# Contextual attention on one core: a third PSUM bank for the paste, other chunk widths, the shifted add on GpSimd, features ahead of masks

## The reference, cut to what matters

```python
raw_w = extract_patches(b, 4, 2)              # 1600 patches of 64 x 4 x 4
f = b[:, :, ::2, ::2]                         # 40 x 40
w = extract_patches(f, 3, 1)                  # 1600 patches of 64 x 3 x 3
mm = (mean of the mask patch == 0)
norm = sqrt(sum(w * w)); wn = w / maximum(norm, 1e-4)
yi = einsum('bpd,bld->blp', w, wn) * mm       # scores, l: patch, p: place
yi = softmax(yi * 10, axis=l) * mm
patches = einsum('blp,bld->bpd', yi, raw_w)
out = overlap-add of the patches with stride 2, cut by 1, / 4
```

## Time and profile before

| | us |
|---|---|
| runs, median (lowest, highest) | 1791.49 (1788.55, 1794.37) |
| profiled execution, its own time | 1782.45 |
| its span | 1780.6 |
| PE busy | 1591.8 |
| DVE busy | 1090.1 |
| ACT busy | 901.4 |
| POOL busy | 51.2 |
| mean granted TensorE clock | 0.952 |

### The profile page before, as it was taken

One profiled execution on the slowest core, in us unless ns is written; L12 is line 12 of the kernel. 1 busy time (PEld: TensorE's weight loads), 2 busy tenths in 40 slices (PEclk: granted clock), 3 DMA queues, 4 the chain that ended last, 5 costly groups with the idle time before them and its releaser, 6 DMA issues.

```text
span 1780.6 us, 27285 instructions
## 1 busy us (share of the span) xinstructions
PE 1591.8 (89%) x7260; PEld 1052.2 (59%) x7260; DVE 1090.1 (61%) x2526; ACT 901.4 (51%) x2265; POOL 51.2 (3%) x62
## 2 busy tenths in 40 slices
PE   3887899998999899998999989999899989999986
PEld 3756566665666566565665656666566656656543
DVE  5224555675566756576656755667556676667784
ACT  1446454574446744565535645457344573457431
POOL 1000100001000000000000010000100000000100
PEclk9987899999999999998999999999889999999998
DMA  3400624226422445225352262422633234522342
GB/s 61 62 1 12 143 61 89 72 70 139 84 63 72 104 111 106 55 69 124 86 96 61 66 145 66 92 72 73 137 71 77 72 94 109 106 64 66 112 122 78
DMA packets 181701, 149.64 MB, mean 84 GB/s; under 512 B 120016, under 2 KB 177424, under 8 KB 181520
## 3 DMA queue, kind: packets, MB, share of 16 engines
q1 hardware_dynamic: 181522, 147.62, 35.1%
HBM read 19.78 MB, written 13.11 MB: 18 GB/s over the span
## 4 chain that ended last, share of the span: by engine, by line
PE 71%; DVE 10%; ACT 8%; issue 7%; SPq 2%; DMA 1%; DVEq 0%; ACTq 0%; POOL 0%; POOLq 0%
PE psG L433 35%; PE psO L449 30%; DVE S L723 4%; ACT S L575 3%; PE psG L428 3%; DVE G L773 2%; PE psM L347 2%; ACT G L565 2%; ACT OSB L595 1%; ACT G L586 1%; PE psB L362 1%; SPq L251 1%; DVE Z L806 1%; DVE G L784 1%; ACT SQ L529 1%
## 5 line engine op out<-in xcount | busy, mean ns | idle before, releaser
L449 PE MATMUL psO<-Z,B 123*128 123x492 f32 (+2 forms) x1792 | 786.5, 569 | 66.7 <-ACT OSB L595 57.9
L723 DVE CUSTOM_DVE_ANT_0 S<-psG,RB 123x369 f32<-123x369 f32 (+1 forms) x448 | 267.4, 605 | 547.3 <-PE psG L433 471.0
L565 ACT ACTIVATE G<-psG 123x369 f32<-123x369 f32 (+1 forms) x448 | 236.6, 529 | 695.8 <-DVE mx L723 693.9
L449 PEld LDWEIGHTS psO<-Z,B 123*128 123x128 f32 x1792 | 335.9, 199 | 301.3 <-issue 202.3
L433 PE MATMUL psG<-LH,HL 128*123 128x369 f16 (+3 forms) x2592 | 474.8, 329 | 26.2 <-issue 13.8
L433 PEld LDWEIGHTS psG<-LH,HL 128*123 128x123 f16 x2592 | 338.0, 138 | 175.3 <-issue 94.9
L586 ACT ACTIVATE G<-G,nb 123x492 f32<-123x492 f32 (+1 forms) x448 | 268.2, 646 | 125.5 <-DVE G L773 125.1
L575 ACT ACTIVATE S<-S,nm 123x360 f32<-123x360 f32 (+3 forms) x560 | 306.3, 551 | 0.1
L773 DVE SCALAR_TENSOR_TENSOR G<-G,RA,psB 123x492 f32<-123x492 f32 (+1 forms) x448 | 275.4, 658 | 21.8 <-issue 18.2
L784 DVE TENSOR_TENSOR G<-G,SH 123x492 f32<-123x492 f32 (+1 forms) x448 | 251.2, 601 | 14.7 <-DMA SH<-G 14.5
L806 DVE TENSOR_TENSOR Z<-G 123x984 f32<-123x984 f32 (+2 forms) x192 | 209.8, 1093 | 30.4 <-PE psO L449 30.3
(11 more groups left out here) (74 smaller groups left out, 515.2 us busy)
## 6 DMA issues: line engine op xcount, KB each, us to landing
SH<-G SPq DMA_DIRECT2D x224, 214.8 KB
SH<-G SPq DMA_DIRECT2D x224, 161.0 KB
XP<-x SPq DMA_DIRECT2D x20, 280.0 KB, 5.5
XP<-mid SPq DMA_DIRECT2D x20, 280.0 KB, 5.4
SH<-G SPq DMA_DIRECT2D x224, 19.2 KB
HL<-SQ SPq DMA_DIRECT2D x16, 246.5 KB, 3.3
LH<-SQ SPq DMA_DIRECT2D x16, 246.5 KB, 4.5
SH<-G SPq DMA_DIRECT2D x224, 14.4 KB
```

The lines of the kernel that those rows point to most:

```text
L449: last = pe.matmul(psO[:, b, 0:n], B[:, o:o + 128], Z[:, 2 * (s % 2) + j, 0:n], start=t == 0, stop=t == TILES - 1)
L565: act.activation(G[:, t * GLEN + c0:t * GLEN + c0 + n], psG[0:TW, par, 0:n], ACT.Copy).then_inc(g_read, 1)
L723: dve.tensor_tensor_reduce(S[:, par, 0:n], psG[0:TW, par, 0:n], RB[:, s0 * TW:s0 * TW + n], 1.0, 0.0, ALU.mult, ALU.max, mx[:, par:par + 1 ...
```

## The change

Chunk widths become 3, 4, 4, 3 for the paste and 2, 4, 4, 4 for the scores. Scores start in slot 3 instead of 2; slots 17, 18 and 21 have two pairs, slots 2, 28 and 29 none. `psO` gets three banks and `psM` one. A chunk's two accumulations use the banks of `O_BANK`; from the second chunk on b = 0 has a bank that is free and b = 1 waits only for the first of the two reads of the chunk before. Between images (chunk 3 to chunk 0) the banks are the same two, and each b waits for its own. `read_out` moves ahead of `softmax_pair`. The patch copies of ACT come one slot later, and all users of `psM` follow one another in its one bank; `scale_rows` is spread over the end of the pass (g = 0) and slots 3, 4 and 5. `add_shifted` moves from DVE to POOL, with no slot of its own: POOL waits for each DMA in turn. On DVE `sum_pair` goes first in a slot. Four feature tensors become one tensor `PK`, and six DMAs lay it out instead of eight. `low_features(0)` goes ahead of the mask work.

```diff
-P_CHUNKS = [(0, 4), (4, 4), (8, 3), (11, 3)]
-S_CHUNKS = [(0, 3), (3, 4), (7, 3), (10, 4)]
+P_CHUNKS = [(0, 3), (3, 4), (7, 4), (11, 3)]
+S_CHUNKS = [(0, 2), (2, 4), (6, 4), (10, 4)]
-AHEAD = 2
 def score_list(s):
-    if s < 16:
-        return [s - FIRST]
-    if s < 21:
-        return [14, 15] if s == 16 else [s - 1]
-    if s < SLOTS:
-        return [20, 21] if s == 21 else [s]
-    return []
+    if s < 3 or s >= SLOTS:
+        return []
+    if s < 17:
+        return [s - 3]
+    if s < 22:
+        return [[14, 15], [16, 17], [18], [19], [20, 21]][s - 17]
+    return [s]
...
-        psO = ps("psO", [128, 2, 512])
+        psO = ps("psO", [128, 3, 512])
-        psM = ps("psM", [128, 2, 512])
+        psM = ps("psM", [128, 512])
+        O_BANK = [(2, 1), (0, 2), (1, 0), (2, 1)]
...
-                for dst, src in ((HL[0:64, :], HS), (HL[64:128, :], LS), (LH[0:64, :], LS), (LH[64:128, :], HS),
-                                 (H1[0:64, :], HS), (H1[64:128, 0:n - 1], HS[:, 1:n]),
-                                 (HV[0:64, :], HS), (HV[64:128, 0:n - TW], HS[:, TW:n])):
+                for dst, src in ((PK[0:64, 0:3, :], HS.unsqueeze(1).to_broadcast([64, 3, n])), (HL[64:128, :], LS),
+                                 (LH[0:64, :], LS), (LH[64:128, :], HS),
+                                 (H1[64:128, 0:n - 1], HS[:, 1:n]), (HV[64:128, 0:n - TW], HS[:, TW:n])):
...
         def scale_rows(u, v, g):
             pe.wait_ge(r_step, (v + 1) * R_STEPS)
-            if g == 0 and u is not None:
+            if g > 0:
                 pe.sem_inc(pe_gate, 1)
-                pe.wait_ge(b_made, u * PAIRS + 4)
-            if g == 2 and u is not None:
+                pe.wait_ge(r_rows, v * 4 + g)
+            elif u is not None:
                 pe.sem_inc(pe_gate, 1)
                 pe.wait_ge(b_made, (u + 1) * PAIRS)
-            if g in (1, 3):
-                pe.sem_inc(pe_gate, 1)
-                pe.wait_ge(r_rows, v * 4 + (1 if g == 1 else 2))
...
         def paste_tile(at, s, j):
-                    if i == 0:
-                        pe.wait_ge(o_read, (u * NK + k + 1) * 2)
...
                 for b in range(2):
+                    if t == 0:
+                        pe.sem_inc(pe_gate, 1)
+                        pe.wait_ge(o_read, (u * NK + k) * 2 + b + (2 if k == 0 else 1))
                     o = (2 * t + b) * 128
-                    last = pe.matmul(psO[:, b, 0:n], B[:, o:o + 128], Z[:, 2 * (s % 2) + j, 0:n],
+                    last = pe.matmul(psO[:, O_BANK[k][b], 0:n], B[:, o:o + 128], Z[:, 2 * (s % 2) + j, 0:n],
                                      start=t == 0, stop=t == TILES - 1)
...
         # ACT, body
-                    at = place(u, v, s + LEAD)
+                    if u is not None and s % PAIRS == 0 and s <= SLOTS:
+                        read_out(u, s // PAIRS - 1)
                     if s == 24 and v is not None:
                         lse_log(v, False)
-                    elif at:
+                    at = place(u, v, s + LEAD)
+                    if at and s != 24:
                         softmax_pair(at)
-                    if u is not None and s % PAIRS == 0 and s <= SLOTS:
-                        read_out(u, s // PAIRS - 1)
+                    if v is not None and (NK - 1) * PAIRS < s <= SLOTS:
+                        block_group(u, v, s - 1 - (NK - 1) * PAIRS)
...
         # DVE, body
+                    at = place(u, v, s + 1)
+                    if at:
+                        sum_pair(at, s + 1)
+                    at = place(u, v, s + LEAD)
+                    if at and s != 24:
                         argument_pair(at)
-                    at_y = place(u, v, s + AHEAD)
-                    if at_y:
-                        add_shifted(at_y)
-                    at_z = place(u, v, s + 1)
-                    if at_z:
-                        sum_pair(at_z, s + 1)
...
         # POOL
+                    pool.wait_ge(sh_in[o % SFREE], (u * (NB // SFREE) + o // SFREE + 1) * 16 * len(SHIFT_PARTS))
+                    g = G[:, t * GLEN + c0:t * GLEN + c0 + n]
+                    pool.tensor_tensor(g, g, SH[:, o % SFREE, 0:n], ALU.add).then_inc(y1_made, 1)
...
             def body(u, v):
                 for s in BODY:
+                    at = place(u, v, s + LEAD)
+                    if at:
+                        add_shifted(at)
```

More of the change, by code:

```diff
@@ L72, in contextual_attention @@
         G = sb("G", [TW, TILES * GLEN], F32)
[L73 to L76, removed]
+        PK = sb("PK", [128, 4, FLEN], F16)
+        HL, H1, HV, LH = (PK[:, i, :] for i in range(4))
         XP = sb("XP", [128, TILES * STRIPS, 2 * PITCH], F32)
@@ L343, in row_squares @@
                 if v is not None:
-                    pe.wait_ge(r_rows, v * 4 + 3)
+                    pe.wait_ge(r_rows, v * 4 + 4)
                 for r in range(FROWS):
-                    last = pe.matmul(psM[0:TW, Q_BANK, r:r + 1], SQ[0:64, r * TW:(r + 1) * TW], ones[:, :],
+                    last = pe.matmul(psM[0:TW, r:r + 1], SQ[0:64, r * TW:(r + 1) * TW], ones[:, :],
                                      start=True, stop=True)
@@ L395, in block_group @@
                     pe.sem_inc(pe_gate, 1)
[L397 to L402, removed]
+                if g > 0:
+                    pe.wait_ge(b_made, v * PAIRS + g)
+                elif w is not None:
+                    pe.wait_ge(r_step, w * R_STEPS + 4)
                 else:
-                    pe.wait_ge(b_made, v * PAIRS + g)
+                    pe.wait_ge(r_rows, v * 4 + 4)
                 for t in (2 * g, 2 * g + 1):
@@ L408, in block_group @@
                         o = (t % 2 * 2 + b) * 128
-                        last = pe.transpose(psM[0:TW, BLOCK_BANK[g], o:o + 128], xt, idn[:, :])
+                        last = pe.transpose(psM[0:TW, o:o + 128], xt, idn[:, :])
                 last.then_inc(blk_psum, 1)
@@ L457, in body @@
                     pairs = score_list(s) if v is not None else []
-                    if s == 4 and v is not None:
-                        scale_rows(u, v, 2)
-                        scale_rows(u, v, 3)
+                    if 3 <= s <= 5 and v is not None:
+                        scale_rows(u, v, s - 2)
                     if s == 5 and u is not None:
@@ L464, in body @@
                         lse_row(u, 3)
-                    if s == FIRST and v is not None:
+                    if pairs and pairs[0] == 0:
                         pe.wait_ge(f_in, (v + 1) * N_F * 16)
@@ L482, in body @@
                         block_group(v, w, s - 21)
-                    if w is not None and s in (25, 26):
-                        scale_rows(v, w, s - 25)
+                if w is not None:
+                    scale_rows(v, w, 0)
                 if v is not None:
@@ L489, in _ @@
             for t in range(TILES):
-                last = pe.matmul(psM[0:TW, 0, 2 * t:2 * t + 2], G[0:LAYERS, MASK_AT + t * TW:MASK_AT + (t + 1) * TW],
+                last = pe.matmul(psM[0:TW, 2 * t:2 * t + 2], G[0:LAYERS, MASK_AT + t * TW:MASK_AT + (t + 1) * TW],
                                  idn[0:LAYERS, 0:LAYERS], start=True, stop=True)
@@ L540, in scale_rows @@
                 n = min(4, TILES - 4 * g) * TW
-                act.activation(RB[:, 4 * g * TW:4 * g * TW + n], psM[0:TW, ROW_BANK[g], 0:n], ACT.Copy).then_inc(r_rows, 1)
+                act.activation(RB[:, 4 * g * TW:4 * g * TW + n], psM[0:TW, 0:n], ACT.Copy).then_inc(r_rows, 1)
             def block_group(u, v, g):
@@ L548, in block_group @@
                 act.wait_ge(blk_psum, v * PAIRS + g + 1)
-                act.activation(B[:, g * 512:(g + 1) * 512], psM[0:TW, BLOCK_BANK[g], :], ACT.Copy).then_inc(b_made, 1)
+                act.activation(B[:, g * 512:(g + 1) * 512], psM[0:TW, :], ACT.Copy).then_inc(b_made, 1)
             def score_pair(u, v, j):
@@ L633, in body @@
                         softmax_pair(at)
-                    if s == 4 and v is not None:
-                        scale_rows(v, 2)
-                        scale_rows(v, 3)
+                    if v is not None and 3 <= s <= 5:
+                        scale_rows(v, s - 2)
                     if w is not None:
@@ L643, in body @@
                             roots(w)
[L644 to L648 removed]
+                if w is not None:
+                    scale_rows(w, 0)
             act.wait_ge(cleared, CLEARED)
@@ L891, in _ @@
             dve.sem_inc(dve_gate, 1)
-            low_features(0)
             column_sums(0)
```

65 lines of the change are left out of this document (24 added, 41 removed).

## The result

The changed kernel takes 1810.25 us (median of four runs, 1805.39 to 1820.9) beside 1790.02 for the kernel before on the same chip: 1.0129 times as long, 95% interval 1.0067 to 1.019. It is 1.3% slower, and the whole interval lies above 1; 1733 was forecast, with a range that ended at 1773. The profiled execution took 1805.39 us, its span 1803.6 against 1780.6.

What follows compares the result with a forecast made beforehand. It took the busiest engine of each slot, plus waits and low clock, as the bound: 212.2 us a pass, 205.2 after. -49 (seven passes) + 2 - 2.5 - 9 = -58 gave 1724, by the median's ratio 1733; range 1697 to 1773.

Steps and rivals of the forecast that it cites:

- The account of a pass: Each of 28 slots costs its busiest engine's work; these plus waits and low clock take a pass from 212.2 to 205.2 us.
- Is the add in time?: GpSimd's add before DVE's neighbour sum: the way takes 8.7 of some 10 us, so it was costed at nothing.
- rival 2: Late GpSimd adds hold DVE's neighbour sum, and behind it arguments, maxima and PE: +28 + 8, 1769 us; chance 0.17.
- What the add costs: Shifted add on GpSimd: 1.3 us estimated, the middle between DVE's 0.63 and a scaled copy's 1.95.
- Rival 1: GpSimd becomes the bound if an add takes 2.5 us: 1838 us, turning at an add of about 2.0; chance 0.09.
- The lock: GpSimd stands while DVE does a neighbour sum, 1.18 us a slot; DVE standing up to 1.3 was left open.
- Third bank: Another `psO` bank cuts the paste's waits for ACT's read-out in slots 7, 14 and 28 from 7.7 to 2.4 us a pass.
- The new wait on `psM`: Scale rows in slots 4 and 5 wait for ACT's copy from the single bank: 1.15 us twice, +2.3 a pass.
- Chunk widths: Paste widths only reordered, no cost; the scores' new tiles, with two transposes fewer, add 1.2 us of PE a pass.
- First pass: Earlier `low_features(0)` starts PE 2.5 us sooner; new waits add 5.6, scores 1.2, the layout wait shrinks 2.5: together +2.
- Last pass: Only paste and its supply, with SP full: 95 us from slot 2 to the end instead of 104, -9.
- the ring: Reading after measurement: late shifts delay GpSimd's add, DVE's sum and the arguments behind it, then later exps, shifts and adds.

## Why the prediction was wrong

*The account of a pass.* PE's work was right: 185.6 us a pass with the new widths, 184.3 with the old, by the median time from start to start of each form in the two unrolled kernels; +1.2 was forecast. What failed is the step from the largest engine of each slot to the sum of slots (192.6 to 190.3, "gain 2.3"). It takes an engine's order in a slot as free. DVE's relief of 169 us was real, and the pass stayed at 211.0, over the 209 above which the prediction called itself wrong. (No run has the sum first and the adds on DVE, so what the relief is worth in that order is not known.)

*"Is the add in time? I cost it at nothing."* This is the step that turned the sign. The way to the add was reckoned at 8.7 us of some 10, with SP's queue at its shifts only. With a store (4 to 5.2 us), a layout (8.2) or feature loads (2.1) in front, the shift is late by more than the 1 us of slack. The prediction named the slack, and rival 2 named the waiting sum with the arguments behind it, but priced it at 1 us in four slots a pass and 0.5 us a slot in the last. One wait there is up to 8.8 us, and it returns through exp, shift and add. Priced by the run that only moves the sum, it is 51 us; rival 2 had 36. The mechanism of the rival was right, and its size and its chance of 0.17 too low. For the new order of DVE, stated in the change, the prediction named no price at all: the slot's sum was only counted as ahead.

*What the add costs.* 1.3 us estimated, 1.1 measured (medians 1.22 at 492 columns and 0.96 at 369). Rival 1, 2.0 us and more, did not come. (Its price is mis-added: 1733 + 54 + 57 makes 1844, not 1838.)

*The lock.* The trace before showed GpSimd standing beside DVE's sum; the other direction was left open. It is seen: sums of 984 columns take up to 2.10 us instead of 1.18 in the changed kernel, and instructions over two numbers a partition up to 1.05 instead of 0.17. Over the kernel L709 went from 38.0 to 49.8 us. The Trainium skill ("SBUF — State Buffer", Who interferes with whom) says that whichever of the two starts first holds the other, and the rows of the sums agree.

*Third bank.* Right: 2.4 us a pass forecast in place of 7.7, and 21.5 in eight, 2.7 each, measured.

*The new wait on `psM`.* Found, and a quarter too small: 2.3 a pass and 5.6 in the first make 22, the run that removes it saves 29, of which 12 before the first slot 28.

*Chunk widths.* "The paste's four widths are only put in another order: no cost" is the other step that failed. As PE's work it is true. But the order decides which slots are short where SP's queue is longest. 22 us hang on it, 15 of which come back when the strip alone is issued earlier. The scores' part, +1.2 a pass, was near: 10 forecast in eight passes, 11 measured.

*Loop turn.* Kept at 2.8, it is 5.2 in the changed kernel: +12 in five turns.

*First pass.* -2.5 forecast for the first score, -0.1 measured (46.7 against 46.8). With the old widths it comes at 44.7, and with these and the new start at 46.7, so the earlier `low_features` did bring 2 us and the new start took them. *Last pass.* -9 forecast, +17.5 measured; with the sum last -4.7.

The sum now: -58 forecast, +20 measured. 51 of the 78 are the ring, 17 the widths beyond their 10 (27 measured with the sum last), 7 the rows. That is near, but the prices overlap, the loop turn's 12 stands in them too, and they were taken in different kernels, so it compares sizes and proves nothing. Inside the two profiles the 23 us between the spans are 20 of idle time on PE, 11 of work, most of it the scores' widths, and 8 fewer for the clock (table below). The parts that were to help did so, by subtraction: the kernel with adds on DVE stands level with the kernel before although it carries about 29 for the rows and 27 for the widths. No run had the third bank alone.

## What to carry to other kernels

Where an engine runs a fixed order, put what waits for the longest chain last in its slot and what feeds that chain first; relief of a busy engine buys nothing by itself: here it was worth 24 us with the sum last beside the third bank, and nothing when it was made alone in the kernel before. Before calling a move of widths free, count the issues in the DMA queue between two points in time and lay them beside the length of the slots there: the shortest slots must not meet the fullest queue. One buffer for several users costs little if the copy that frees it is first in its slot.

## What the runs showed of the hardware

**DVE and GpSimd hold each other in both directions**, and a tiny instruction is held about as long as a large one. In the changed kernel DVE's sums of 984 columns take up to 2.10 us instead of 1.18, its instructions over two numbers a partition up to 1.05 instead of 0.17. With the adds moved in the kernel before, a GpSimd add takes 2.64 instead of 1.05, and a DVE copy of 64 x 82 takes 1.12 instead of 0.19.

**The turn of a hardware loop.** PE's idle time at the turn, with nothing to release it, in the changed kernel:

```profile
634.14 5.14 PE L438 MATMUL psO<-Z,B 123*128 123x369 f32 x8 [4.71 <-issue]
```

A turn costs 2.8 us in the kernel before and 3.7 with the old widths and the sum last, where a score tile comes first behind it. It costs 5.2 in the changed kernel and 5.7 with the sum last, where a paste tile does. In the kernel before too SP issues DMAs around the turn (a store from 630.87 to 635.69, the turn ending at 632.16). What makes the difference stays open.

Writing the loops out is worth 28 us in the kernel before, twice its 13.8 us of turns. The paste's idle time is not where they come from. Looped and written out:

```profile
L449 PE MATMUL psO<-Z,B 123*128 123x492 f32 (+2 forms) x1792 | 786.5, 569 | 66.7 <-ACT OSB L595 57.9 <-DVE Z L806 4.7 <-issue 3.9
L449 PE MATMUL psO<-Z,B 123*128 123x492 f32 (+2 forms) x1792 | 783.0, 567 | 66.9 <-DVE Z L806 29.3 <-issue 27.6 <-ACT OSB L595 9.9
```

The releasers have other names, but the waits are the old ones: 3.94 us in each slot 28 with "issue" for what was 3.89 for `OSB`, and ACT's read-out ends just before PE starts in both. The next entry has what does make the 28 us.

**PE's idle time and TensorE's clock give the time of all these kernels.** Of each profile: the span, PE's idle time, the time at a granted clock of 1.2 GHz instead of 2.4, and what is left of the span after the idle time and half of the low-clock time.

| kernel | span | PE idle | at 1.2 GHz | left |
|---|---|---|---|---|
| before | 1780.6 | 182.1 | 169.9 | 1513.6 |
| before, unrolled | 1752.5 | 167.7 | 141.6 | 1514.0 |
| changed | 1803.6 | 201.9 | 154.2 | 1524.6 |
| sum last | 1753.7 | 169.5 | 120.6 | 1523.9 |
| unrolled, new widths | 1717.5 | 140.9 | 102.6 | 1525.3 |
| unrolled, new, strip first | 1700.2 | 131.5 | 78.6 | 1529.4 |
| unrolled, new scores, old paste | 1689.3 | 123.5 | 77.4 | 1527.1 |
| unrolled, old widths | 1678.5 | 123.6 | 79.6 | 1515.1 |

What is left is 1514 to 1515 with the scores' old widths and 1524 to 1529 with the new: PE's own work and its 11 us more. All else is idle time and the clock. Half of the low-clock time is an estimate from the two levels, and too much where it falls on idle time: with the adds moved and the sum first in the kernel before (span 1856.8, 244.8 idle, 232.6 at 1.2 GHz) 1496 is left. Unrolling the kernel before saves 14 us of idle time, the turns, and 14 by the clock; putting the sum last saves 32 and 17 of the changed kernel's 50. A gap closed was worth 1.5 to 2 times its length in these two.
